# Two halves of a batch: layer by layer in turns, with each norm made inside the other half's layer, against one half after the other

## What is computed

```python
x = x + alpha * single_head(x, context)
for l in (1, 2):
    h = layer_norm(x) * scale_l + offset_l
    q, k, v = h @ wq + bq, context @ wk + bk, context @ wv + bv      # 16 heads of 128
    k, v = [k, bias_k], [v, bias_v]
    x = x + softmax(q k^T / sqrt(128)) v @ wo + bo
h = layer_norm(x) * scale_m + offset_m
out = x + gelu(h @ w_fc1 + b_fc1) @ w_fc2 + b_fc2
```

## Time and profile before

| | us |
|---|---|
| median of 3 runs (lowest, highest) | 1818.28 (1815.3, 1818.33) |
| the profiled execution: its time | 1822.36 |
| its span | 1820.6 |
| PE busy | 1796.2 |
| DVE busy | 1155.7 |
| POOL busy | 759.4 |
| ACT busy | 731.6 |

### The profile page before, as it was taken

How to read it: one execution, slowest core, us unless ns; L and a number is a source line. 1 busy time by engine, 2 the same in 40 slices (tenths; PEclk the granted TensorE clock), 3 DMA queues, 4 the chain that set the end, 5 groups by cost and what they waited for, 6 DMA issues and landing times.

```text
span 1820.6 us, 30822 instructions
## 1 busy us (share of the span) xinstructions
PE 1796.2 (99%) x11460; PEld 1754.2 (96%) x11460; DVE 1155.7 (63%) x2748; ACT 731.6 (40%) x1644; POOL 759.4 (42%) x621
## 2 busy tenths in 40 slices
PE   8999999999999999999999999999999999999999
PEld 5899999999999999999999999999999999999999
DVE  3667666666675665666687666566676566666665
ACT  3634333333343333343475333333334333334354
POOL 2674352352261353530488245252255252352244
PEclk9999999999999999999999999999999999999999
DMA  8833231121221222210473112121032121121232
GB/s 258 236 113 90 66 86 40 49 70 33 59 74 30 55 59 51 77 46 9 152 216 95 39 40 80 45 66 51 13 88 54 39 78 39 43 76 33 61 113 83
DMA packets 107511, 136.87 MB, mean 75 GB/s; under 512 B 47968, under 2 KB 59488, under 8 KB 107364
## 3 DMA queue, kind: packets, MB, share of 16 engines
q1 hardware_dynamic: 104644, 130.60, 25.5%
q10 hardware_dynamic: 2720, 4.30, 0.7%
HBM read 132.19 MB, written 2.68 MB: 74 GB/s over the span
## 4 chain that ended last, share of the span: by engine, by line
PE 91%; DVE 4%; DMA 2%; ACT 1%; POOL 1%; issue 1%; SPq 0%; DVEq 0%; ACTq 0%
PE psum L619 28%; PE psum L620 27%; PE psum L621 27%; PE psum L914 4%; PE psum L653 2%; DMA ctx_rows_in<-ctx_dram 1%; PE psum L790 1%; PE psum L808 1%; DVE xT L1587 1%; PE psum L632 1%; PE psum L628 1%; DVE h_lo L1386 0%; PE psum L629 0%; DVE psum L1555 0%; DMA key_stage<-head_w_dram 0%
## 5 line engine op out<-in xcount | busy, mean ns | idle before, releaser
L511 POOL TENSOR_TENSOR wbuf_hi<-stage,zero_col 128x512 fp32r<-128x512 f32 x256 | 267.9, 1047 | 919.2 <-PE psum L621 610.4
L555 POOL TENSOR_TENSOR wbuf_lo<-stage,wbuf_hi 128x512 fp32r<-128x512 f32 x256 | 330.5, 1291 | 20.0
L619 PE MATMUL psum<-pT_hi,ctx_rows_hi 121*128 121x250 f32 (+3 forms) x1152 | 331.4, 288 | 0.0
L621 PE MATMUL psum<-pT_hi,ctx_rows_lo 121*128 121x250 f32 (+3 forms) x1152 | 331.4, 288 | 0.0
L620 PE MATMUL psum<-pT_lo,ctx_rows_hi 121*128 121x250 f32 (+3 forms) x1152 | 331.0, 287 | 0.0
L619 PE MATMUL psum<-ctxT_hi,a_hi 128*125 128x362 f32 (+1 forms) x832 | 280.3, 337 | 0.4
L1382 DVE TENSOR_TENSOR a_lo<-psum,a_hi 128x500 fp32r<-128x500 f32 (+2 forms) x288 | 146.1, 526 | 211.9 <-ACT a_hi L1035 211.7
L621 PE MATMUL psum<-ctxT_hi,a_lo 128*125 128x362 f32 (+1 forms) x832 | 272.8, 328 | 0.0
L620 PE MATMUL psum<-ctxT_lo,a_hi 128*125 128x362 f32 (+1 forms) x832 | 272.7, 328 | 0.0
L619 PE MATMUL psum<-a_hi,wbuf_hi 128*128 128x400 f32 x720 | 254.6, 354 | 1.7 <-DVE xT L1587 1.6
L620 PE MATMUL psum<-a_lo,wbuf_hi 128*128 128x400 f32 x720 | 247.6, 344 | 0.0
(11 more groups left out here) (180 smaller groups left out, 3408.9 us busy)
## 6 DMA issues: line engine op xcount, KB each, us to landing
stage<-head_w_dram SPq DMA_DIRECT2D x256, 256.0 KB, 2.6
mlp_stage<-mlp_w_dram SPq DMA_DIRECT2D x32, 512.0 KB, 3.7
p_b<-p_scratch SPq DMA_DIRECT2D x64, 200.0 KB, 3.6
ctx_rows_in<-ctx_dram SPq DMA_DIRECT2D x12, 726.0 KB
ctxT_in<-ctxT_dram SPq DMA_DIRECT2D x12, 724.0 KB, 9.0
key_stage<-head_w_dram SPq DMA_DIRECT2D x22, 256.0 KB, 8.6
l0w<-l_w_dram ACTq DMA_DIRECT2D x16, 256.0 KB, 8.8
p_scratch<-p_row ACTq DMA_DIRECT2D x192, 0.5 KB
```

What stands on the lines that cost most here:

```text
L511: return nc.gpsimd.tensor_tensor(out, in_, zero_col[0:in_.shape[0], :].broadcast_to(tuple(in_.shape)), ALU.add)
L555: nc.gpsimd.tensor_tensor(lo, held, hi.bitcast(F32), ALU.subtract).then_inc(stage_free, 1)
L619: pe.matmul(out, a_h, x_hi, start=start, stop=False)
L621: return pe.matmul(out, a_l, x_hi, start=False, stop=stop)
```

## The change

The phases now run as layer 0 of half 0, layer 0 of half 1, layer 1 of half 0, layer 1 of half 1, and then the two MLPs. In each phase the norm that the next phase (or the first MLP) needs is made inside ("hidden"): the other half's `x` is loaded from a DRAM tensor `x_d` into `x_held` when q15 is done; POOL sums its four chunks, PE makes the mean with one matmul, DVE centres, ACT squares, POOL sums again, PE makes the variance with one matmul; the rest is placed between the last pieces. At the end of each of the first three phases SP stores `xT` (800 KB) into `x_d`, waits, and loads the other half's into `xT`. The context's buffers are given to the other half at these three edges: reload and split of 4 + 4 transfers each time, where before it was done once, in the first MLP. Only the first norm, and in the second MLP the products in pieces of a norm spread over the first MLP, stay as they were. The core of the diff:

```diff
+PHASES = [(half, l) for l in range(LAYERS) for half in range(HALVES)]
+MEAN_IN, SQUARES_IN, X_BEHIND = (LAST_UNIT, 1), (LAST_UNIT, 2), 56
+SUMS_BEHIND = 57
+ROWS_LO_BEHIND = {9: 1, 10: 2, 11: 3}
...
 # SP
+            early = WBUFS + STAGES
+            for ph, (half, l) in enumerate(PHASES):
+                last = ph == len(PHASES) - 1
+                sp.wait_ge(s0_row, ph + 1)
...
+                for i in range(early, W_AT["v", H - 1]):
...
+                    load_weights(ph, i)
...
+                    if i == X_BEHIND:
+                        sp.wait_ge(y_mm, ph * R_LAYER + R_AT["q", H - 1] + 1)
+                        sp.wait_ge(x_st, ph * 16 + 16)
+                        sp.dma_start(x_held[:, :, :], x_d[1 - half]).then_inc(hn_ld, 16)
+                if not last:
+                    for b in range(NB - 1):
+                        reload_ctx_columns(ph, b)
+                        reload_ctx_rows(ph, b)
+                    reload_ctx_columns(ph, NB - 1)
+                load_weights(ph, W_AT["v", H - 1])
+                for h in (H - 4, H - 3, H - 2):
+                    load_first_probs(ph, h)
+                load_weights(ph, W_AT["o", H - 3])
+                if not last:
+                    reload_ctx_rows(ph, NB - 1)
+                load_weights(ph, W_AT["o", H - 2])
+                load_first_probs(ph, H - 1)
+                load_weights(ph, W_AT["o", H - 1])
+                if not last:
+                    for i in range(early):
+                        load_weights(ph + 1, i)
+                    sp.wait_ge(y_done, (ph + 1) * R_LAYER)
+                    sp.dma_start(x_d[half], xT[:, :, :]).then_inc(x_st, 16)
+                    sp.wait_ge(x_st, ph * 16 + 32)
+                    sp.dma_start(xT[:, :, :], x_d[1 - half]).then_inc(x_back, 16)
 # POOL
+                    split_weights(ph, i)
+                    if ph > 0 and i in ROWS_LO_BEHIND:
+                        ctx_rows_lo(ph + TURNS - 1, ROWS_LO_BEHIND[i])
+                    if i == SUMS_BEHIND:
+                        hidden_x_sum(ph)
+                        hidden_square_sum(ph)
+                        if ph + 1 < len(PHASES):
+                            ctx_rows_lo(ph + TURNS, 0)
 # PE
+                def hidden_mean():
+                    out = free_bank("n", 0)
+                    pe.wait_ge(hn_sum, ph * 2 + 1)
+                    pe.matmul(out[:, 0:N], mean_w[:, :], centred[:, 0, :], start=True, stop=True).then_inc(hn_mean, 1)
...
+                else:
+                    queries_of_hidden(0)
+                    bias_scores()
+                    queries(1)
...
+                if again:
+                    pe.wait_ge(hn_lo, len(PHASES) * DC)
+                    hidden(0)
+                    hidden(1)
+                    mean_sums(LAST_NORM, xT, lambda c: pe.wait_ge(y_done, len(PHASES) * R_LAYER))
 # ACT
                 send_first_row(*before, len(UNITS[before[0]]) - 1)
+                hidden_roots(ph)
                 attended_hi(*before)
-                run_pieces("end")
+                if reload:
+                    ctx_columns_hi(ph + TURNS, 1)
+                for kind, h in pieces("end"):
+                    if kind == "v":
+                        values_hi(h)
+                    if (kind, h) == ("v", H - 3) and reload:
+                        ctx_rows_hi(ph + TURNS, 1)
+                    if (kind, h) == ("v", H - 2):
+                        hidden_hi(ph)
+                if reload:
+                    ctx_columns_hi(ph + TURNS, 2)
+                    ctx_rows_hi(ph + TURNS, 2)
 # DVE
                         maxima(k, b, 1)
                         normalise(k, b, 1)
+                        if (k, b) == MEAN_IN:
+                            hidden_centre(ph)
+                        if (k, b) == STEPS[-1] and reload:
+                            ctx_columns_lo(ph + TURNS, 0)
+                        if k == 0 and b < 2 and ph > 0:
+                            ctx_columns_lo(ph + TURNS - 1, b + 2)
...
                 run_pieces("last split")
-                attended_lo(*before)
-                run_pieces("end")
+                hidden_invert(ph, 0, 2)
+                attended_lo(*before, 0, 2)
+                hidden_invert(ph, 2, NB)
+                attended_lo(*before, 2, DC)
+                for kind, h in pieces("end"):
+                    (values_lo if kind == "v" else add_output)(h)
+                    if (kind, h) == ("v", H - 4) and reload:
+                        ctx_columns_lo(ph + TURNS, 1)
+                    if (kind, h) == ("v", H - 3):
+                        hidden_scale(ph, 0, 2)
+                    if (kind, h) == ("v", H - 2):
+                        hidden_scale(ph, 2, DC)
+                    if (kind, h) == ("v", H - 1):
+                        hidden_low(ph, 0, 2)
+                    if (kind, h) == ("o", H - 3):
+                        hidden_low(ph, 2, DC)
```

More of the change, by code:

```diff
@@ L121, in made_in_order @@
     for k, b in STEPS:
-        order += products((k, b, "a")) + products((k, b, "m")) + before + products((k, b, "b"))
+        order += products((k, b, "a")) + products((k, b, "m")) + [("n", 0)] * ((k, b) == MEAN_IN)
+        order += before + products((k, b, "b"))
         before = attended(k, b)
@@ L128 @@
 M_AT = {made: i for i, made in enumerate(MADE)}
+MADE_LAYER = len(MADE)
 MBUFS = 5
@@ L502, in _, with store_outputs @@
+            def store_outputs(half):
                 for m in range(DC):
@@ new lines, in _ @@
+            for ph in range(len(PHASES)):
+                for i in range(W_LAYER):
+                    if ph == 0 and i == WBUFS - 1:
+                        pool.wait_ge(kw_sum, KEYS_BEFORE)
+                    split_weights(ph, i)
[6 more added lines that the diff above has]
+                            ctx_rows_lo(ph + TURNS, 0)
@@ L615, in _ @@
+            w1_low(0)
+            w2_low(0)
+            w1_low(1)
+            for k in range(HALVES * FB):
+                if k + 2 < HALVES * FB:
+                    w1_low(k + 2)
+                if k + 1 < HALVES * FB:
+                    w2_low(k + 1)
         @block.tensor
@@ L850, in first_queries, with queries_of_hidden @@
                 def first_queries(h, n):
                     hi, lo = weights("q", h)
-                    done = product_of_norm(output("q", h)[:, piece(n)], lambda c: chunk(hi, c), lambda c: chunk(lo, c), j, n)
+                    done = product_of_norm(output("q", h)[:, piece(n)], lambda c: chunk(hi, c), lambda c: chunk(lo, c), FIRST_NORM, n)
                     if n == 1:
                         done.then_inc(y_mm, 1)
+                def queries_of_hidden(h):
+                    hi, lo = weights("q", h)
+                    out = output("q", h)
+                    for c in range(DC):
+                        pe.wait_ge(hn_lo, (ph - 1) * DC + c + 1)
+                        mm = mm3(out, chunk(hi, c), chunk(lo, c), h_hi[:, c, :], h_lo[:, c, :], start=(c == 0),
+                                 stop=(c == DC - 1))
+                    mm.then_inc(y_mm, 1)
@@ L1023, in mlp_block @@
                     if again and fb == SQUARES_AFTER:
-                        square_sums(BETWEEN)
+                        square_sums(LAST_NORM)
             single_head()
+            for ph in range(len(PHASES)):
+                layer(ph)
             for half in range(HALVES):
-                for l in range(LAYERS):
-                    layer(half, l)
                 mlp_block(half)
@@ L1269, in layer @@
                 queries_hi(1)
-                wait(act, landed, half * (DC * 16) + 16)
+                act.wait_ge(x_st, 16)
                 run_pieces("start", 2)
@@ L1311, in layer @@
                             send_first_row(k, b, 1)
+                        if (k, b) == STEPS[-2] and reload:
+                            ctx_columns_hi(ph + TURNS, 0)
                     before = k, b
```

454 lines of the change are left out of this document (242 added, 212 removed).

## The result

The changed kernel takes 1833.3 us (median of 5 runs, 1826.7 to 1835.1), the kernel before 1818.3 beside it: ratio **1.0072 (1.0055 to 1.0089)**, slower by 13 us by this ratio (15.0 by the medians), where 5 us less had been forecast, and outside the range. Its profiled execution took 1826.7 with a span of 1824.9. The mean granted clock of its five runs is 0.993, 0.991, 0.991, 0.989 and 0.988, and their times rise in about that order; the kernel before has 0.999 or 1.000 in most runs.

What follows compares the result with a forecast made beforehand. PE was taken as the bound (busy 1796.2 of 1820.6 us). Removing 43.4 and adding 2.7 gains 40.7; 35.5 go back, leaving 5.2: median 1818.3 becomes 1813.1. Own range 1804 to 1822; with rivals 1793 to 1829.

Steps and rivals of the forecast that it cites:

- the clock's term: Loss from PE's clock dropping at the ends of phases; taken as nothing in the forecast sum.
- the clock falls at the edges: Rival: PE's clock drops at four edges, half of 6.8 us each, 13.6 in all: 1827; chance 0.06.
- The gain of 43.4: PE time removed at layer edges, the turn between halves and both MLPs by hiding norms: 43.4 us.
- DVE at the end of a phase: DVE's added work from v12 to q0 delays PE: 6.0 us at three edges, 3.7 at the fourth, 21.7 total.
- The exchange: Storing and reloading x in SP's queue delays q3's weights: 1.1 us at three edges, 3.3 total.
- The rival of a slow exchange: x's store takes 7.3 and the bias row waits for the whole reload; q3 6.4 us late: 1829; chance 0.15.
- Context columns of batch 2: DVE's split in a phase's first step lengthens PE's wait at the second turn: 6.9 us for three.
- Means: PE's mean for the hidden norm waits on x's load and POOL's sums: 0.9 us late four times, 3.6.
- Added matmuls: Mean and variance on PE for four norms: 8 matmuls of 400 columns, 0.34 each, 2.7 us.
- Faster if the edges cost 2 instead of 6: Rival: DVE keeps up at the ends of phases, an edge costing 2 us instead of 6: 1799.4; chance 0.27.
- that rival with free means and exchange: DVE keeps up, and the mean's lateness and x's store and reload (6.9 us) cost nothing: 1792.5.
- its upper bound of 30 for DVE: Worst case for DVE's delay at phase ends: 3.47 us for the context split and twice the 1.4 for low parts.

Runs made afterwards that it cites:

- e12_before_unfilled: Kernel before the change, without the matmuls that only keep PE busy at the norms made in the open; ratio 1.0011.
- e8_busy_less: Changed kernel plus useless 128-column matmuls in PE's waits at each edge: 6 before v15, 3 in o15, 9 before the second turn; ratio 1.0019.
- e3_busy: Changed kernel plus useless 128-column matmuls in five waits per edge: 8 before v15, 3 and 6 in o14 and o15, 5 before q3, 13 before the second turn; 1.0037.
- e2_columns_in_start: Changed kernel with DVE's context splits of batches 1 and 2 moved behind q0 and q1 of the next phase; ratio 0.9976, 1814.4 us.
- e6_gaps: e4_both with the hidden norm's four DVE scalings moved into DVE's waits at v12 to v15, and ACT's order changed; ratio 0.9952, 1811.1 us.
- e9_spread: e6_gaps plus POOL's context-row splits in thirds, its sum of x earlier, and the norm's four low parts placed singly; ratio 0.9847, 1791.0 us.
- e4_both: e2_columns_in_start plus SP's queue reordered: bias row and q3's weights first, store and reload of x later; ratio 0.9982.

## Why the prediction was wrong

**The step that failed** is the clock's term, put at nothing in the sum and kept as the rival "the clock falls at the edges". Its price came out about right for the profiled execution: half of 6.8 per edge, 13.6 for four; the trace has up to 13.6, at three edges (27.2 us at 1.2 GHz). For the median run it was too low. That its 1827 meets the profiled execution's 1826.7 is luck, since it was a forecast of the median; the profiled one would have been 1831. Its chance was put at 0.06, on two grounds. The clock went down "at none of the norms": but there matmuls that do nothing fill PE's waits, which the prediction itself had read from the busy 16.53 of 16.60, and without them it does fall now and then (e12_before_unfilled). And it had been low only "once": the forecast's own sum put waits of 6.0, 1.1 and 3.4 us at the end of a phase, at q3 and at the second turn, without anything to fill them, and did not ask what the clock would do there. e8_busy_less shows the sign and most of the size: filling alone gives back 9.6 of 13 us, within 4.

**The median** lies another 6.6 above the profiled execution, whose clock (0.993) was the highest of the five. Between 0.999 and 0.990 lies a half-clock share worth up to 16 us of 1830; 4.7 gained and up to 16 lost is up to 12, and 13 was measured (15.0 by the medians). How many falls an execution has differs from run to run, and this kernel's times spread over 8 us with it. Not all of the spread need be the clock: e3_busy's five runs at 1.000 lie between 1817.4 and 1823.8.

**The other steps**, point by point. The gain of 43.4 came where it was put: from q0 to k0 of the next layer it is 6.55 us (510.87 to 517.42), as forecast, and from the first hidden product to the first output product of the two MLPs 6.9 and 7.0, where 7.1 and 6.6 were taken. DVE at the end of a phase: right in place and size, 19.0 for 21.7; its parts were tested by e2_columns_in_start, e6_gaps and e9_spread. The exchange: 4.6 for 3.3, inside its bounds; the store took 4.4, near the 4.7 taken. The rival of a slow exchange (1829) gave nearly the measured time for a reason that did not occur. Context columns of batch 2: 6.5 for 6.9. That POOL's instruction holds DVE was weighed only for the context split and the low parts of h; its larger effect here, POOL's row splits on the probabilities, was behind the split's own wait and showed only when that was gone (e4_both). Means: the sum of 3.2 for 3.6 is partly luck, since the mean was late once (0.9) and not four times, and the other three gaps are the hold of DVE's scaling. Added matmuls: mis-sized by 2, 5.4 for 2.7. "Faster if the edges cost 2 instead of 6" was not the case. e9_spread comes to its size, 1791, where that rival with free means and exchange gave 1792.5; but its edits also take away the second turn's added wait, which the rival kept. Two slips in the prediction's own figures change nothing: its upper bound of 30 for DVE adds up to 30.9, and a quarter of 0.40 above 1814.6 would leave 0.30 of it for "faster", not 0.26.

**What stays open.** Why the clock falls in one stretch and not in another was not separated from where a wait falls: e8_busy_less holds 1.00 in an edge with PE busy for 58.97 of 65, e2_columns_in_start has 0.97 with 59.60. And whether the changed kernel at full clock would be faster than the one before: the trace's balance says 4.7, the fillings' own cost hides it in the runs.

## What to carry to other kernels

When a change replaces work on TensorE by short waits, price the clock with the waits: ask of every stretch that looks safe what PE did in it, and count matmuls that only keep it busy as protection that the change removes. The cheap test is to fill the waits with useless matmuls: if the kernel gets faster, the clock was the cost; then take the waits away. And when a wait is removed and the time stays, look at what the next instruction on that engine is held by before giving up the edit; here the second of two edits gained nothing (e4_both against e2_columns_in_start), and 9 us came once POOL's long instruction was cut. Whether they would have come without that second edit was not run.

## What was not expected of the hardware

Adding 18 matmuls of 128 columns per edge shortened the kernel by 9.6 us. A DVE scaling of 125 x 362 numbers with one SBUF input, 0.41 us alone, took up to 2.90 beside a POOL instruction of 3.48, and 0.57 to 0.96 beside POOL instructions of 1.3. DVE held POOL in the same way: a weight's `wbuf_hi` of 1.04 took 2.47 beside the context split of 2.19. And a store of 25 KB queued behind a reload of 800 KB took 3.9 us, against 1.5 in the kernel before.
